# Channel mask of the last token group added by TensorE, in an adaLN attention and sparse-FFN kernel

## What is computed

```python
h = layernorm(x) * (1 + ca) + sa
x = x + ga * attention(h)                 # causal, one head of 128, softmax, Wo, bo
h = layernorm(x) * (1 + cb) + sb
prob = softmax(h @ w_router + b_router)   # 16 blocks of 32 hidden channels
mask = top 4 of 16 blocks, per token
hid = relu(h @ w1.T + b1)                 # 512 hidden channels
x = x + gb * (sum over chosen blocks of hid @ w2.T + b2)
```

## Time and profile before

| | us |
|---|---|
| median of 3 runs (124.83 to 124.90) | 124.84 |
| profiled execution, its own time | 124.88 |
| span of the profiled execution | 123.1 |

### The profile page before, as it was taken

How to read it: one execution, slowest core, us unless ns; L and a number is a source line. 1 busy time by engine, 2 the same in 40 slices (tenths; PEclk the granted TensorE clock), 3 DMA queues, 4 the chain that set the end, 5 groups by cost and what they waited for, 6 DMA issues and landing times.

```text
span 123.1 us, 2048 instructions
## 1 busy us (share of the span) xinstructions
PE 113.1 (92%) x616; PEld 91.2 (74%) x616; DVE 92.7 (75%) x307; ACT 75.5 (61%) x163; POOL 87.2 (71%) x123
## 2 busy tenths in 40 slices
PE   6999768999999999999998999969998999989880
PEld 2476656988888888888985888858896888867670
DVE  0489779889999999988988391953489866797941
ACT  2235589556948195797638998786932479426630
POOL 7788886733999079897698699997796489844000
PEclk9999999999999999999999999999999999999999
DMA  2994000000000000000000000000000002003032
GB/s 56 253 283 137 0 3 3 5 0 0 0 3 0 0 5 0 0 0 0 0 3 0 5 0 0 0 0 0 5 0 0 3 0 85 3 0 91 0 85 85
DMA packets 6273, 3.42 MB, mean 28 GB/s; under 512 B 1140, under 2 KB 5877, under 8 KB 6262
## 3 DMA queue, kind: packets, MB, share of 16 engines
q1 hardware_dynamic: 5830, 3.09, 8.9%
q10 hardware_dynamic: 432, 0.20, 0.5%
HBM read 2.24 MB, written 1.05 MB: 27 GB/s over the span
## 4 chain that ended last, share of the span: by engine, by line
PE 57%; DVE 16%; POOL 11%; issue 6%; ACT 5%; DMA 3%; POOLq 1%; DVEq 0%; ACTq 0%
PE bank L774 14%; PE bank L770 13%; PE bank L771 13%; PE bank L817 6%; DVE keys L674 5%; PE bank L877 3%; DMA cols<-in_L_c_dram 3%; POOL rstd L364 3%; DVE hid_full L697 2%; POOL hid_lo L436 2%; DVE chosen L688 2%; DVE marked L683 2%; ACT hid_hi L539 2%; PE bank L794 1%; ACT xn L495 1%
## 5 line engine op out<-in xcount | busy, mean ns | idle before, releaser
L430 POOL TENSOR_TENSOR p_lo<-p_full,p_hi 128x512 fp32r<-128x512 f32 (+3 forms) x40 | 44.3, 1128 | 14.2 <-ACT p_full L523 14.0
L516 ACT ACTIVATE p_hi<-bank 128x512 fp32r<-128x512 f32 (+3 forms) x40 | 21.6, 541 | 11.9 <-PE bank L774 6.4
L523 ACT ACTIVATE p_full<-bank 128x512 f32<-128x512 f32 (+3 forms) x40 | 21.6, 540 | 0.2 <-POOL p_lo L430 0.2
L436 POOL TENSOR_TENSOR hid_lo<-hid_full,hid_hi 128x512 fp32r<-128x512 f32 x12 | 15.4, 1288 | 4.7 <-ACT hid_hi L539 4.7
L611 DVE TENSOR_REDUCE cmax<-bank 128x1 f32<-128x512 f32 x24 | 16.3, 687 | 1.5 <-PE bank L817 1.0
L817 PE MATMUL bank<-zt_hi,g_hi 128*128 128x512 f32 (+3 forms) x40 | 15.5, 401 | 0.5 <-DVE g_hi L637 0.3
L539 ACT CAST hid_hi<-hid_full 128x512 fp32r<-128x512 f32 x16 | 9.9, 620 | 9.7 <-DVE hid_full L697 9.5
L697 DVE SCALAR_TENSOR_TENSOR hid_full<-bank,keep 128x512 f32<-128x512 f32 x16 | 10.9, 689 | 5.9 <-POOL hid_lo L436 2.5
L770 PE MATMUL bank<-g_hi,zt_hi 128*128 128x512 f32 (+3 forms) x40 | 15.1, 377 | 0.0
L770 PE MATMUL bank<-p_hi,z_hi 128*128 128x512 f32 (+3 forms) x40 | 15.0, 376 | 0.0
L771 PE MATMUL bank<-p_hi,z_lo 128*128 128x512 f32 (+3 forms) x40 | 14.6, 365 | 0.0
(11 more groups left out here) (165 smaller groups left out, 257.7 us busy)
## 6 DMA issues: line engine op xcount, KB each, us to landing
x<-in_L_attn_y_all_dram SPq DMA_DIRECT2D x4, 256.0 KB, 4.0
out_dram<-res SPq DMA_DIRECT2D x3, 256.0 KB, 2.3
w<-in_L_ffn_w_dram SPq DMA_DIRECT2D x2, 256.0 KB, 3.9
wmod<-in_L_wmod_dram SPq DMA_DIRECT2D x1, 256.0 KB, 4.7
out_dram<-res SPq DMA_DIRECT2D x2, 128.0 KB, 1.8
wmod<-in_L_wmod_dram ACTq DMA_DIRECT2D x1, 128.0 KB, 3.7
wk<-in_L_attn_Wk_dram SPq DMA_DIRECT2D x1, 64.0 KB, 3.3
wq<-in_L_attn_Wq_dram ACTq DMA_DIRECT2D x1, 64.0 KB, 3.4
```

The source lines that it names most:

```text
L430: pool.tensor_tensor(p_lo[:, s, w:], p_full[:, n % 2, w:], p_hi[:, s, w:].bitcast(F32), ALU.subtract).then_inc(p_lo_pool, 1)
L436: pool.tensor_tensor(hid_lo[:, m, :], hid_full[:, n % 2, :], hid_hi[:, m, :].bitcast(F32), ALU.subtract).then_inc(hid_lo_pool, 1)
L516: nc.scalar.activation(p_hi[:, s, w:], src, ACT.Exp).then_inc(p_hi_s, 1)
L523: nc.scalar.activation(p_full[:, n % 2, w:], src, ACT.Exp).then_inc(p_full_s, 1)
```

## The change

The router's keys become max(lmax - 87.33, logit) in one SCALAR_TENSOR_TENSOR for all four tiles, with pads and marks of 3e38 in place of 1.0 (two comparisons in `choose` change with it). For the last group (`shut_by_tensor`), VectorE writes the 16 blocks not chosen as 128x4x16 bf16; TensorE turns that to 16 rows of 512 tokens; ScalarE copies 16x512; and a new step `v` on TensorE adds, in a fourth matmul of each hidden chunk, `spread` (16x128, -1e30 where a channel belongs to the block) times these 16 rows. ScalarE then takes relu out of the PSUM bank into `hid_hi`, and VectorE takes relu minus `hid_hi` out of the same bank into `hid_lo`; L697 is gone for these four chunks. The router's sums of the last group go to `score_bank[0]`, its four high matmuls first, which wait for the high half of the tokens alone. GpSimd builds `spread` within its step z4. All four plans are rearranged.

```diff
@@ -32 +32 @@
...
 SCALAR_NORMS = (1, 2, 3, 4, 5, 6, 7)
-VECTOR_HALVES = (12, 13, 14, 15)
+VECTOR_HALVES = ()
 HIDES_FROM = 1
...
 TENSOR_PLAN = """
-z0 i0 i1 i2 i3 i4 z1 i5 i6 i7 i8 i9 i10 i11 i12 z2 i13 i14 i15 i16 i17 i18 n0 z3 i19 q0 i20 i21 i22 n1 a0 a1
-i23 a2 q1 a3 n2 a4 b0 z4 a5 a6 s0 a7 a8 z5 s1 s2 a9 s3 a10 q2 a11 w0 n3 a12 b1 w1 a13 w2 w3 a14 s4 s5 a15 s6
-a16 z6 a17 s7 s8 a18 s9 a19 z7 a20 z8 w4 s10 a21 a22 w5 q3 a23 s11 w6 a24 w7 b2 w8 a25 w9 w10 a26 s12 a27 s13
-w11 o0 s14 s15 w12 o1 z9 s16 w13 s17 a28 w14 a29 s18 a30 w15 a31 n4 s19 a32 a33 w16 s20 a34 s21 a35 w17 a36
-w18 a37 s22 a38 r0 a39 s23 w19 w20 b3 h0 w21 w22 s24 w23 s25 s26 s27 m0 w24 s28 n5 o2 w25 s29 s30 w26 s31 s32
-w27 r1 s33 s34 w28 w29 w30 s35 m1 s36 s37 w31 h1 s38 h2 w32 n6 h3 w33 s39 w34 r2 w35 w36 w37 w38 w39 h4 d0 m2
-o3 d1 d2 d3 h5 h6 d4 y0 h7 h8 d5 n7 h9 d6 h10 r3 d7 h11 d8 h12 y1 m3 d9 h13 d10 h14 d11 h15 y2 d12 d13 d14 d15
-d16 d17 d18 d19 y3 y4
+i0 i1 i2 z0 i3 i4 i5 i6 i7 z1 i8 i9 i10 i11 i12 i13 i14 i15 z2 i16 i17 i18 i19 i20 i21 n0 z3 i22 q0 i23 i24
+i25 n1 a0 a1 i26 a2 q1 a3 n2 a4 b0 z4 a5 a6 s0 a7 s1 a8 z5 a9 n3 s2 a10 s3 a11 w0 q2 w1 b1 w2 a12 z6 w3 a13 s4
+a14 s5 a15 z7 a16 s6 a17 s7 a18 z8 w4 a19 s8 a20 w5 a21 q3 a22 s9 s10 a23 a24 w6 w7 b2 w8 s11 a25 w9 a26 s12
+w10 o0 s13 w11 z9 s14 a27 a28 s15 s16 s17 o1 s18 w12 s19 a29 a30 w13 s20 a31 w14 a32 w15 a33 s21 a34 n4 a35
+w16 a36 s22 w17 a37 w18 a38 w19 s23 a39 r0 w20 b3 w21 w22 h0 w23 s24 s25 s26 h1 m0 s27 w24 s28 s29 n5 w25 s30
+w26 o2 s31 w27 s32 w28 s33 r1 h2 w29 w30 s34 w31 s35 w32 s36 m1 h3 s37 n6 h4 w33 s38 s39 w34 w35 r2 w36 w37
+w38 w39 h5 d0 m2 o3 d1 d2 d3 h6 h7 y0 h8 d4 d5 h9 n7 d6 h10 d7 r3 h11 d8 h12 d9 m3 d10 y1 v12 h13 v13 d11 h14
+v14 h15 v15 y2 d12 d13 d14 d15 d16 d17 d18 d19 y3 y4
 """
 SCALAR_PLAN = """
-z0 z1 z3 n0 a1 q0 n1 a2 q1 n2 z4 a3 e0 z5 e1 q2 e2 e3 n3 e4 e5 e6 z6 c0 e7 z7 e8 e9 q3 e10 z8 e11 e12 e13 c1
-e14 e15 a4 e16 e17 n4 e18 a5 e19 e20 e21 e22 e23 e24 c2 e25 m0 e26 e27 n5 e28 e29 e30 e31 e32 e33 e34 e35 h0
-m1 a6 h1 e36 n6 e37 e38 h2 h3 e39 c3 h4 m2 y0 h5 h6 a7 h7 n7 h8 h9 y1 h10 h11 m3 h12 h13 y2 h14 h15 y3 y4
+z0 z1 z3 n0 a1 q0 n1 a2 q1 n2 a3 z4 e0 z5 e1 n3 e2 q2 e3 z6 c0 e4 e5 z7 e6 z8 e7 q3 e8 e9 e10 e11 e12 e13 e14
+c1 e15 e16 e17 a4 e18 e19 n4 e20 e21 e22 a5 e23 c2 e24 e25 e26 m0 e27 e28 h0 e29 e30 n5 h1 e31 e32 e33 h2 a6
+e34 m1 e35 e36 n6 e37 e38 e39 h3 c3 h4 h5 y0 m2 h6 a7 h7 h8 n7 y1 h9 h10 h11 m3 h12 h13 y2 h14 h15 y3 y4
 """
 VECTOR_PLAN = """
-g0 z1 g1 a0 g2 z3 n0 z10 g3 q0 s0 n1 s1 s2 s3 q1 s4 b0 s5 s6 n2 s7 s8 z5 s9 s10 s11 s12 b1 s13 n3 s14 q2 s15
-z11 s16 s17 s18 i8 s19 z6 s20 z7 i9 s21 s22 i10 s23 s24 b2 s25 i11 s26 s27 q3 z8 x0 g4 x1 g5 s28 z9 s29 s30
-s31 n4 s32 s33 s34 s35 s36 i20 s37 i21 s38 s39 i22 i23 b3 m0 c0 h0 x2 n5 g6 m1 c1 i36 i37 h1 i38 n6 h2 i39 h3
-m2 c2 h4 x3 g7 h5 h6 f0 h7 h8 n7 h9 h10 m3 c3 h11 f1 h12 h13 k12 k13 h14 h15 k14 k15 f2 f3 f4
+g0 z1 g1 a0 g2 z3 n0 z10 g3 q0 s0 n1 s1 s2 s3 q1 s4 b0 s5 s6 n2 s7 s8 s9 z5 s10 s11 n3 z11 b1 s12 q2 s13 s14
+s15 z6 s16 s17 z7 s18 s19 s20 i8 s21 s22 i9 s23 i10 s24 b2 s25 s26 i11 z8 x0 s27 z9 s28 g4 x1 g5 s29 s30 i20
+s31 s32 s33 s34 i21 s35 i22 s36 n4 s37 s38 s39 i23 q3 b3 m0 c0 h0 h1 x2 n5 g6 m1 h2 c1 i36 h3 i37 h4 n6 i38
+i39 m2 c2 h5 x3 g7 h6 h7 h8 n7 h9 h10 m3 c3 h11 f0 f1 k12 k13 k14 k15 f2 f3 f4
 """
 GPSIMD_PLAN = """
-z2 z0 z5 z7 p0 z8 z1 p1 u0 p2 u1 p3 z6 l0 l1 l2 l3 l4 l5 l6 u2 l7 l8 l9 l10 l11 l12 l13 z4 l14 p4 l15 p5 l16
-l17 l18 l19 l20 l21 l22 l23 u3 l24 l25 l26 l27 l28 l29 l30 l31 l32 l33 p6 l34 l35 k0 l36 k1 l37 l38 l39 k2 k3
-k4 p7 k5 k6 k7 k8 k9 k10 k11
+z2 z0 z4 z5 z1 p0 z8 p1 u0 p2 u1 z7 p3 z6 l0 l1 l2 l3 l4 u2 l5 l6 l7 l8 l9 l10 u3 l11 l12 l13 l14 l15 p4 l16
+l17 p5 l18 l19 l20 l21 l22 l23 l24 l25 l26 l27 l28 k0 l29 l30 l31 p6 l32 k1 l33 l34 k2 l35 l36 l37 l38 l39 k3
+k4 k5 p7 k6 k7 k8 k9 k10 k11
 """
...
@@ -196 +196 @@
+
+        shut_by_tensor = (NG - 1,)
+        shut, spread = sb("shut", [NBLK, GW], BF16), sb("spread", [NBLK, P], BF16)
+        spread_full = sb("spread_full", [NBLK, P])
+        unchosen = sb("unchosen", [P, GT, NBLK], BF16)
@@ -271 +276 @@
...
         def vector_halves(n):
-            return n in VECTOR_HALVES
+            return n in VECTOR_HALVES or n // NH in shut_by_tensor
...
@@ -301 +306 @@
...
             return (ctx_bank, score_bank[2], ctx_bank, score_bank[2], score_bank[0])[n]
+
+        def sums_bank(g):
+            return norm_bank if g < NG - 1 else score_bank[0]
...
@@ -422 +430 @@
...
                 elif i == 4:
-                    pool.memset(keys[:], 1.0).then_inc(keys_made, 1)
+                    pool.memset(keys[:], FURTHEST).then_inc(keys_made, 1)
+                    step(pool.memset(spread_full[:], FAR))
+                    step(pool.affine_select(out=spread_full[:], in_=spread_full[:], compare_op=ALU.is_ge, fill=0.0, base=0,
+                                            pattern=[[1, P]], channel_multiplier=-PER))
+                    step(pool.affine_select(out=spread_full[:], in_=spread_full[:], compare_op=ALU.is_ge, fill=0.0,
+                                            base=PER - 1, pattern=[[-1, P]], channel_multiplier=PER))
+                    pool.tensor_copy(spread[:], spread_full[:]).then_inc(spread_made, 1)
...
@@ -530 +544 @@
...
                 act.wait_ge(chosen_turned, g + 1)
-                nc.scalar.copy(grp(keep, g), norm_bank[:, 0:GW // 2].bitcast(BF16)).then_inc(keep_s, 1)
+                if g in shut_by_tensor:
+                    nc.scalar.copy(shut[:], norm_bank[0:NBLK, 0:GW // 2].bitcast(BF16)).then_inc(keep_s, 1)
+                else:
+                    nc.scalar.copy(grp(keep, g), norm_bank[:, 0:GW // 2].bitcast(BF16)).then_inc(keep_s, 1)
...
             def hidden(n):
-                act.wait_ge(turn_out, turn_of[f"h{n}"] + 1)
+                by_tensor = n // NH in shut_by_tensor
+                act.wait_ge(turn_mm if by_tensor else turn_out, turn_of[f"h{n}"] + 1)
                 if n >= NH:
                     act.wait_ge(y_mm, n - NH + 1)
+                if by_tensor:
+                    nc.scalar.activation(hid_hi[:, n % NH, :], turned_bank(f"h{n}")[:], ACT.Relu).then_inc(hid_hi_s, 1)
+                    return
                 nc.scalar.copy(hid_hi[:, n % NH, :], hid_full[:, n % 2, :]).then_inc(hid_hi_s, 1)
...
@@ -664 +685 @@
...
             def logits(g):
+                sums = sums_bank(g)[:, 0:GT * 2 * NBLK].rearrange("p (i s e) -> p i s e", i=GT, s=2)
                 dve.wait_ge(logits_mm, g + 1)
...
                     dve.wait_ge(keys_made, 1)
-                sums = norm_bank[:, 0:GT * 2 * NBLK].rearrange("p (i s e) -> p i s e", i=GT, s=2)
                 step(nc.vector.tensor_reduce(logit[:], sums.rearrange("p i s e -> p i e s"), AX.X, ALU.add))
                 step(nc.vector.tensor_reduce(lmax[:], logit[:], AX.X, ALU.max))
-                for i in range(GT):
-                    last = nc.vector.tensor_scalar(keys[:, i, 0:NBLK], logit[:, i, :], lmax[:, i:i + 1], UNDER, ALU.subtract, ALU.max)
-                last.then_inc(keys_s, 1)
+                most = lmax[:].rearrange("p (i o) -> p i o", o=1).broadcast_to([P, GT, NBLK])
+                nc.vector.scalar_tensor_tensor(out=keys[:, :, 0:NBLK], in0=most, scalar=UNDER, in1=logit[:], op0=ALU.add,
+                                               op1=ALU.max).then_inc(keys_s, 1)
...
@@ -680 +701 @@
...
                 for i in range(GT):
-                    last = nc.vector.match_replace(marked[:, i, :], top8[:, i, :], keys[:, i, :], 1.0)
+                    last = nc.vector.match_replace(marked[:, i, :], top8[:, i, :], keys[:, i, :], FURTHEST)
                 step(last)
+                if g in shut_by_tensor:
+                    nc.vector.tensor_scalar(unchosen[:], marked[:, :, 0:NBLK], FURTHEST, None, ALU.is_lt).then_inc(chosen_s, 1)
+                    return
                 if g >= 1:
...
                 each = marked[:, :, 0:NBLK].rearrange("p i (e o) -> p i e o", o=1).broadcast_to([P, GT, NBLK, PER])
-                nc.vector.tensor_scalar(chosen[:], each, 0.0, None, ALU.is_gt).then_inc(chosen_s, 1)
+                nc.vector.tensor_scalar(chosen[:], each, FURTHEST, None, ALU.is_ge).then_inc(chosen_s, 1)
...
@@ -700 +724 @@
...
                 dve.wait_ge(hid_hi_s, n + 1)
+                if n // NH in shut_by_tensor:
+                    nc.vector.scalar_tensor_tensor(out=hid_lo[:, m, :], in0=turned_bank(f"h{n}")[:], scalar=0.0,
+                                                   in1=hid_hi[:, m, :].bitcast(F32), op0=ALU.max,
+                                                   op1=ALU.subtract).then_inc(hid_lo_dve, 1)
+                    return
                 nc.vector.tensor_tensor(hid_lo[:, m, :], hid_full[:, n % 2, :], hid_hi[:, m, :].bitcast(F32),
...
@@ -879 +908 @@
...
             def router(g):
+                halves = wr_halves[:].rearrange("p s e -> p (s e)")
+                sums = [sums_bank(g)[:, i * 2 * NBLK:(i + 1) * 2 * NBLK] for i in range(GT)]
```

(41 more changed lines are left out.)

## The result

| | before | changed |
|---|---|---|
| median, us | 124.87 (124.83 to 124.99, 4 runs) | 123.75 (123.72 to 124.02, 4 runs) |
| span of the profiled execution, us | 123.1 | 122.0 |

The ratio is 0.9914, interval 0.9897 to 0.9931: 1.1 us faster. The forecast was 2.1 us, 122.8.

The account below looks back on a forecast made before the run. TensorE, busy 92% of the span, was taken as the bound, so its standstills and work count. Start +0.2, middle -1.8 and tail -0.5 sum to -2.1 on 124.88: 122.8 us, range 121.7 to 124.3.

Parts of the forecast that it names:

- the tail: Last group, up to d16: four added `v` matmuls against waits and VectorE work taken away; -0.5 us.
- the start: GpSimd's z4 ahead of the silu and z7 ahead of p3 delay both; partly filled by moved work, +0.2 us.
- the middle: TensorE's three mask-transpose waits, 2.6 us, shrink through shorter keys and more cover; -1.8 us.
- rival 2: All waits go: middle -2.6, tail -0.8, start 0, giving 121.5 us; chance 0.12.
- The added cover: Between r1 and m1, 8 blocks instead of 6, 5.6 us, against a router chain of about 4.4.
- The expected rests at m0 and m2: Waits of TensorE still left at the first and third mask transposes: 0.3 and 0.5 us.
- rival 1: GpSimd bounds l29 to l39, or the start's delay stays: 0.5 to 1.5 us lost, 123.8 us; chance 0.19.
- four `v`: Added TensorE matmuls of 512 bf16 columns in the last group, at most 0.23 us each: +0.9 us.
- m3's wait of 0.64: TensorE's wait at the last group's mask transposes before the change, counted as gone: -0.6 us.
- h14, y2, d14, d15: TensorE's tail waits of 0.17, 0.43 and 0.5 us, expected to go as their halves are ready: -1.1 us.
- rival 4: Matmuls of 16 rows stop TensorE 10 times, 0.17 to 0.36 us each: slower, 125.5 us; chance 0.08.
- my own step on the keys: Router, all groups: one keys instruction waits for GpSimd once, up to 1.29 us; saves 0.4, or 1.3 at group 1.

Follow-up runs that it names:

- keys_only: The kernel before with only the one-instruction keys and their pads and marks, plans and masks as before: 122.37 us, ratio 0.9795 to before.
- best: The changed kernel with logits and marked keys in PSUM, and `shut` and `spread` on 128 rows, zeros beyond 16: 122.52 us, ratio 0.9808 to before.
- no_v: The changed kernel without the four `v` matmuls, so the last group goes unmasked (only to price the mask): 121.96 us, ratio 0.9764 to before.
- v_128_rows: The changed kernel with the four `v` matmuls reading 128 rows instead of 16, zeros beyond 16, still bf16: 123.40 us, ratio 0.9893 to before.

## Why the prediction came out as it did

Direction and range held (121.7 to 124.3); the gain was half of the forecast, and the step that failed is the tail. That the time stayed well inside the range is in part luck: the tail was 1.5 us worse than forecast and the start 0.3, and the middle 0.8 better, for a reason to which the forecast gave only a part.

- **The start**, forecast +0.2, was about +0.5: s4 began at 28.53; before, TensorE was at the same point at 27.61 (a14, which stood between, now follows s4). 0.36 us of z6 are done earlier, which leaves 0.56; and of the middle's 2.57, 2.04 are left at r3. The silu began at 5.22 and p3 at 18.04, as forecast, and z5 waited 0.45. GpSimd's two moves do make this delay (with both undone s4 begins at 27.72), but they aren't what the time hangs on: the time is then the same, since GpSimd's added 1.3 us come back between 40 and 56 us. How much of the 0.5 the rest of the new plan brings was not separated.
- **The middle**, forecast -1.8, was about -2.6: all three waits went, as in rival 2. The added cover, to which I gave a part, isn't needed: keys_only gains the same 2.57 on the old plan. The expected rests at m0 and m2 (0.3, 0.5) didn't come, and GpSimd, late next by rival 1, held nothing there.
- **The tail**, forecast -0.5, was +0.99. Term by term, by distances in the timelines (a normal step behind y's four transposes is 0.41, before v12 it was 0.60, of which 0.10 is v's own side; d12 to y3 takes 2.90 us, before 3.50):

| term | forecast | measured |
|---|---|---|
| four `v` | +0.9 | 4 x 0.52 = +2.1 |
| v12 waits for `shut` | +0.4 | about +0.1 |
| m3's wait of 0.64 | -0.6 | about 0 (0.67 before, 0.70 now) |
| m3's transposes to 16 partitions | 0 | +0.1 |
| h14, y2, d14, d15 | -1.1 | -1.2 |
| sum | -0.4 (taken as -0.5) | +1.1 (by r3 to d16: +0.99) |

The two failed terms are the price of `v` (1.2 us) and m3's wait (0.7). For `v` I had taken the distance of full matmuls, and the 16 rows were rival 4's mechanism, to which I gave 0.08. It is real, but smaller than its price of 0.17 to 0.36 a stop: `v` costs 0.29 too much for its two sides, and the transposes to 16 partitions 0.11 behind them (108.22 to 108.54, against 107.46 to 107.67 in keys_only); where nothing is waited for, as in best, there is 0.10 ahead of them too (107.59 to 107.92). With 4 x 0.29 + 0.11 = 1.3 us in place of 2.7, it cost half of the gain and not all. For m3 I had counted VectorE's chain free of GpSimd, as 2.7 us behind r3 (it took some 3.5, from 104.62 to the end of `unchosen` at 108.17), though my own step on the keys said "it can wait once, up to 1.29"; I used that bound for the middle and not for the tail.
- Of the signs named: no wait at the second and third group, L721 (before L697) 12 times and no wait at d14 and d15 came as said. One keys instruction a group came too, of 0.22 to 1.17 us. "Spacing of 0.23 between a `v` and its neighbours" was wrong (0.33 and 0.31), and so was d16 nearer to r3. A slip besides: the 117.90 that the text calls d16 is d17; d16 began at 117.54 before.
- That v's wait would be bought back by relu on ScalarE and one hop less came true in part: d12 follows without a wait, but no_v, v_128_rows and best all show h14's weight load held by the low half (idle for 0.2 to 0.3 us, of which TensorE loses a part).

## What to carry to other kernels

Of a change in several parts, time each part alone: one edit of a few lines here gained 2.5 us, and what came with it gave 1.4 back. On a router chain beside a busy GpSimd, count for each small VectorE instruction whether it reads SBUF alone and can be held for GpSimd's whole instruction; fewer instructions mean fewer holds, and a freed one hands the hold to the next, until the last of them has its input in PSUM. Before moving a mask onto TensorE with few rows, price it with what stands on both its sides, or pad it to 128 rows.
